# Two bias rows of a fused attention kernel: ScalarE copies into the PSUM banks in place of TensorE products with ones

## The reference

```python
qkv = x @ Wqkv.T + bqkv                       # here x is xn
q, k, v = jnp.split(qkv, 3, axis=-1)
...
scores = mask + scale * jnp.einsum('bnd,bmd->bnm', q, k)
attn = jax.nn.softmax(scores, axis=-1)
out = jnp.einsum('bnm,bmd->bnd', attn, v)
...
return out @ Wproj.T + bproj
```

## Time and profile before

| | us |
|---|---|
| median of 3 runs | 1820.19 |
| the profiled execution, its own time | 1821.34 |
| its span, first to last instruction | 1819.5 |
| TensorE (PE) busy | 1688.2 (93%), 8188 products |
| VectorE (DVE) busy | 1669.2 (92%) |
| GpSimd (POOL) busy | 1244.1 (68%) |
| ScalarE (ACT) busy | 787.5 (43%) |

### The profile page before, as it was taken

One profiled execution on the slowest core, in us unless ns is written; L12 is line 12 of the kernel. 1 busy time (PEld: TensorE's weight loads), 2 busy tenths in 40 slices (PEclk: granted clock), 3 DMA queues, 4 the chain that ended last, 5 costly groups with the idle time before them and its releaser, 6 DMA issues. The chain is left out here.

```text
span 1819.5 us, 26315 instructions
## 1 busy us (share of the span) xinstructions
PE 1688.2 (93%) x8188; PEld 823.3 (45%) x8188; DVE 1669.2 (92%) x1636; ACT 787.5 (43%) x1562; POOL 1244.1 (68%) x744
## 2 busy tenths in 40 slices
PE   3799999999999899999999999999999999999955
PEld 3344444444444444444444444444444444444422
DVE  4369999999999999999999999999999999999994
ACT  3544444444444444444444444444444434444311
POOL 3335858768585776958577586857759586776947
PEclk7899999999999999999999999999999999999977
DMA  6000111111111111111111111111111111110000
GB/s 231 1 1 24 35 47 36 47 37 41 41 36 48 36 47 35 47 37 35 47 36 47 37 36 47 36 48 36 42 41 41 43 35 47 36 47 18 26 21 29
DMA packets 40907, 75.33 MB, mean 41 GB/s; under 512 B 4912, under 2 KB 4912, under 8 KB 40752
## 3 DMA queue, kind: packets, MB, share of 16 engines
q1 hardware_dynamic: 40752, 73.43, 12.2%
HBM read 39.85 MB, written 33.55 MB: 40 GB/s over the span
## 5 line engine op out<-in xcount | busy, mean ns | idle before, releaser
L376 POOL TENSOR_TENSOR prod_pv<-kv,probs 128x2048 f32<-128x2048 f32 x192 | 811.2, 4237 | 130.1 <-DVE o_nat L677 117.4
L677 DVE TENSOR_REDUCE o_nat<-prod_pv 128x256 f32<-128x2048 f32 (+1 forms) x192 | 433.2, 2282 | 20.6 <-POOL prod_pv L376 11.9
L632 DVE TENSOR_REDUCE scores<-prod_qk 128x64 f32<-128x2048 f32 x192 | 439.3, 2288 | 7.3
L628 DVE TENSOR_TENSOR prod_qk<-q_ps,kv 128x2048 f32<-128x2048 f32 x192 | 431.9, 2249 | 0.0
L347 POOL TENSOR_TENSOR rstd<-var_eps,minus_half 128x1 f32<-128x1 f32 x128 | 70.3, 549 | 383.9 <-ACT var_eps L430 383.8
L451 ACT ACTIVATE kv<-v_ps 128x512 f32<-128x512 f32 x128 | 142.0, 1110 | 177.0 <-PE v_ps L504 177.0
L411 ACT ACTIVATE xT_hi<-xT_ps 128x512 f16<-128x512 f32 x128 | 76.4, 597 | 319.1 <-PE xT_ps L527 319.1
L504 PE MATMUL q_ps<-wqkv_hi,xT_hi 128*128 128x512 f16 x512 | 201.2, 393 | 0.0
L504 PE MATMUL q_ps<-wqkv_lo,xT_hi 128*128 128x512 f16 x512 | 200.9, 392 | 0.0
L504 PE MATMUL proj_ps<-wproj_hi,oT_hi 128*128 128x512 f16 x516 | 200.7, 389 | 0.0
L504 PE MATMUL proj_ps<-wproj_lo,oT_hi 128*128 128x512 f16 x516 | 200.7, 389 | 0.0
(11 more groups left out here) (136 smaller groups left out, 2461.6 us busy)
## 6 DMA issues: line engine op xcount, KB each, us to landing
xs<-in_L_attn_x SPq DMA_DIRECT2D x128, 256.0 KB, 2.6
out<-xs SPq DMA_DIRECT2D x128, 256.0 KB, 2.0
kv<-in_L_attn_Wqkv SPq DMA_DIRECT2D x3, 1024.0 KB, 10.2
kv<-in_L_ffn_weight SPq DMA_DIRECT2D x1, 1024.0 KB, 5.5
kv<-in_L_attn_Wproj SPq DMA_DIRECT2D x1, 1024.0 KB, 14.3
prod_pv<-in_L_attn_bqkv SPq DMA_DIRECT2D x2, 256.0 KB, 10.3
prod_pv<-in_L_attn_bproj SPq DMA_DIRECT2D x1, 256.0 KB, 9.3
prod_pv<-in_L_ffn_bias SPq DMA_DIRECT2D x1, 256.0 KB, 8.2
```

Of the source, the lines that this page charges most:

```text
L376: nc.gpsimd.tensor_tensor(o, v, p, ALU.mult).then_inc(pv_multiplied, 1)
L628: nc.vector.tensor_tensor(prod_qk[:, :].rearrange("p (m c) -> p m c", c=C), qb, k, ALU.mult).then_inc(qk_multiplied, 1)
L632: nc.vector.tensor_reduce(scores[:, :, m0:m0 + 4].rearrange("p h m -> p m h"), prod_qk[:, :].rearrange("p (m h d) -> p m h d", h=H, d=D), ...
L677: nc.vector.tensor_reduce(o_nat[:, n % 2, h * D:(h + heads) * D], prod_pv[:, u % 2, :].rearrange("p (c m) -> p c m", m=keys), AX_X, ALU.ad ...
```

## The change

The biases of the keys and the queries are no longer split into rows on GpSimd. They are loaded into two fp32 tiles of their own, `k_bias` and `q_bias`, and scaled there. ScalarE copies them into the banks (128 x 512 fp32, SBUF to PSUM), and TensorE's 12 products are added to what the bank holds. Three products in slot 5 (`banks_opened`) open the three banks once. The copy for the queries of slot j is ScalarE's first instruction of the slot, with the wait for `shifted_ready` that TensorE had; the copy for the next tile's keys stands behind the copy of the values out of their bank. The output bias keeps its row of ones.

```diff
-            nc.gpsimd.memset(k_bias_rows[:, :], 0.0).then_inc(consts_set, 1)
-            nc.gpsimd.memset(q_bias_rows[:, :], 0.0).then_inc(consts_set, 1)
...
-            nc.gpsimd.tensor_scalar(bk_all, bk_all, scale[:, 0:1], 1.0, ALU.mult, ALU.mult).then_inc(bias_steps, 1)
-            pool.wait_ge(bias_steps, 1)
-            split_into_rows(bk_all, k_bias_rows, 1, 0)
+            nc.gpsimd.tensor_scalar(k_bias[:, :], k_bias[:, :], scale[:, 0:1], 1.0, ALU.mult, ALU.mult).then_inc(k_bias_ready, 1)
             pool.wait_ge(bq_loaded, 16)
-            nc.gpsimd.tensor_scalar(bq_all, bq_all, scale[:, 0:1], 1.0, ALU.mult, ALU.mult).then_inc(bias_steps, 1)
-            pool.wait_ge(bias_steps, 7)
-            split_into_rows(bq_all, q_bias_rows, 7, 3)
+            nc.gpsimd.tensor_scalar(q_bias[:, :], q_bias[:, :], scale[:, 0:1], 1.0, ALU.mult, ALU.mult).then_inc(q_bias_ready, 1)
...
             def slot(i, j):
                 if at(i, j, L_TRANS):
                     high_parts(2 * KC, N_PARTS)
+                if at(i, j, L_KV):
+                    act.wait_ge(banks_opened, 1)
+                    act.wait_ge(k_bias_ready, 1)
+                    nc.scalar.activation(k_ps[:, :], k_bias[:, :], ACT.Copy).then_inc(k_preset, 1)
+                    act.wait_ge(q_bias_ready, 1)
+                if live(i, j, L_Q):
+
+                    n = j - L_Q
+                    after(act, shifted_ready, tile_count(i, n - 2))
+                    nc.scalar.activation(q_ps[n % 2][:, :], q_bias[:, :], ACT.Copy).then_inc(q_preset, 1)
                 if live(i, j, L_TRANS):
...
                     nc.scalar.activation(v_all[:, g % 2, :, n % N], v_ps[:, :], ACT.Copy).then_inc(v_kept, 1)
+                if live(i, j, L_KV) and live(i, j + 1, L_KV):
+                    after(act, k_kept, tile_count(i, j - L_KV))
+                    nc.scalar.activation(k_ps[:, :], k_bias[:, :], ACT.Copy).then_inc(k_preset, 1)
                 if live(i, j, L_SOFT):
...
             def slot(i, j):
                 if at(i, j, L_KV):
                     pe.wait_ge(w_ready, N_PARTS)
-                    pe.wait_ge(bias_rows_ready, 3)
+
+                    for b in (k_ps, *q_ps):
+                        last = nc.tensor.matmul(b[:, :], wqkv_hi[:, 0, 0:P], wqkv_hi[:, 0, 0:512], start=True, stop=True)
+                    last.then_inc(banks_opened, 1)
...
-                    after(pe, k_kept, tile_count(i, n - 1))
-                    nc.tensor.matmul(k_ps[:, :], ones[:, :], k_bias_rows[:, :], start=True, stop=False)
-                    split_products(k_ps, t_hi, t_lo, wqkv_hi, wqkv_lo, C, first=False).then_inc(k_summed, 1)
+                    after(pe, k_preset, tile_count(i, n))
+                    split_products(k_ps, t_hi, t_lo, wqkv_hi, wqkv_lo, C, first=False, preset=True).then_inc(k_summed, 1)
...
-                    after(pe, shifted_ready, tile_count(i, n - 2))
-                    nc.tensor.matmul(acc[:, :], ones[:, :], q_bias_rows[:, :], start=True, stop=False)
+                    after(pe, q_preset, tile_count(i, n))
                     split_products(acc, xT_hi[:, n % N, :], xT_lo[:, n % N, :], wqkv_hi, wqkv_lo, 0,
-                                   first=False).then_inc(q_summed, 1)
+                                   first=False, preset=True).then_inc(q_summed, 1)
```

More of the change, by code:

```diff
@@ L112, in attention_and_fp8_linear @@
         wffn_q = sb("wffn_q", [P, KC, C], BF16)
-        q_bias_rows = sb("q_bias_rows", [P, C], BF16)
-        k_bias_rows = sb("k_bias_rows", [P, C], BF16)
+        q_bias = sb("q_bias", [P, C], F32)
+        k_bias = sb("k_bias", [P, C], F32)
         out_bias_rows = sb("out_bias_rows", [P, C], BF16)
@@ L171, in attention_and_fp8_linear @@
         diagonals = kv[:, 15872:16064].bitcast(BF16).rearrange("p (a n) -> p a n", n=P)
-        bq_all, bk_all, bo_all, bffn_all = (prod_pv[:, 0, k * C:(k + 1) * C] for k in range(4))
+        bo_all, bffn_all = (prod_pv[:, 0, k * C:(k + 1) * C] for k in range(2))
         bias_rest = prod_pv[:, 1, 0:C]
@@ L195, in attention_and_fp8_linear @@
         bias_rows_ready = sem("bias_rows_ready")
+        k_bias_ready = sem("k_bias_ready")
+        q_bias_ready = sem("q_bias_ready")
+        banks_opened = sem("banks_opened")
+        k_preset, q_preset = (sem(n) for n in ("k_preset", "q_preset"))
         out_biases_scaled = sem("out_biases_scaled")
@@ L267, in _ @@
             sp.dma_start(bqkv_nat[:, :], bqkv.rearrange("(p j) -> p j", p=P)).then_inc(bqkv_loaded, 16)
-            sp.dma_start(bk_all, bqkv[C:2 * C].partition_broadcast(P)).then_inc(bk_loaded, 16)
-            sp.dma_start(bq_all, bqkv[0:C].partition_broadcast(P)).then_inc(bq_loaded, 16)
+            sp.dma_start(k_bias[:, :], bqkv[C:2 * C].partition_broadcast(P)).then_inc(bk_loaded, 16)
+            sp.dma_start(q_bias[:, :], bqkv[0:C].partition_broadcast(P)).then_inc(bq_loaded, 16)
             with nc.allow_non_contiguous_dma(reason="512 numbers, once"):
@@ L303, in _, with split_into_rows @@
                                            bass.bass_isa.ReduceOp.max).then_inc(amax_ready, 1)
-            def split_into_rows(b, rows, steps, ready):
+            def split_into_rows(b, rows):
                 hi, mid, low = bias_parts
                 nc.gpsimd.tensor_copy(hi, b).then_inc(bias_steps, 1)
-                pool.wait_ge(bias_steps, steps + 1)
+                pool.wait_ge(bias_steps, 2)
                 nc.gpsimd.tensor_tensor(bias_rest, b, hi, ALU.subtract).then_inc(bias_steps, 1)
-                pool.wait_ge(bias_steps, steps + 2)
+                pool.wait_ge(bias_steps, 3)
@@ L313, in split_into_rows @@
                 nc.gpsimd.tensor_copy(mid, bias_rest).then_inc(bias_steps, 1)
-                pool.wait_ge(bias_steps, steps + 3)
+                pool.wait_ge(bias_steps, 4)
                 nc.gpsimd.tensor_tensor(bias_rest, bias_rest, mid, ALU.subtract).then_inc(bias_steps, 1)
-                pool.wait_ge(bias_steps, steps + 4)
+                pool.wait_ge(bias_steps, 5)
                 nc.gpsimd.tensor_copy(low, bias_rest).then_inc(bias_steps, 1)
-                pool.wait_ge(bias_steps, steps + 5)
@@ L319, in split_into_rows @@
-                pool.wait_ge(consts_set, 6)
+                pool.wait_ge(bias_steps, 6)
+                pool.wait_ge(consts_set, 4)
                 for k, part in enumerate((hi, mid, low)):
                     nc.gpsimd.tensor_copy(rows[32 * k:32 * k + 1, :], part[32 * k:32 * k + 1, :]).then_inc(bias_rows_ready, 1)
-                    pool.wait_ge(bias_rows_ready, ready + k + 1)
+                    pool.wait_ge(bias_rows_ready, k + 1)
             pool.wait_ge(scales_ready, 1)
             pool.wait_ge(bk_loaded, 16)
-            nc.gpsimd.tensor_scalar(bk_all, bk_all, scale[:, 0:1], 1.0, ALU.mult, ALU.mult).then_inc(bias_steps, 1)
@@ L333, in _ @@
             pool.wait_ge(out_biases_loaded, 32)
             nc.gpsimd.tensor_tensor(bo_all, bo_all, bffn_all, ALU.add).then_inc(bias_steps, 1)
-            pool.wait_ge(bias_steps, 13)
+            pool.wait_ge(bias_steps, 1)
             nc.gpsimd.tensor_scalar(bo_all, bo_all, out_unscale[:, 0:1], 1.0, ALU.mult,
@@ L341, in slot @@
                     pool.wait_ge(out_bias_summed, 1)
-                    split_into_rows(bo_all, out_bias_rows, 13, 6)
+                    split_into_rows(bo_all, out_bias_rows)
                 if live(i, j, L_NORM):
@@ L498, in _, with split_products @@
                 last.then_inc(w_transposed, 1)
-            def split_products(acc, t_hi, t_lo, w_hi, w_lo, col, first=True):
+            def split_products(acc, t_hi, t_lo, w_hi, w_lo, col, first=True, preset=False):
                 parts = [(t, w, c) for c in range(KC) for t, w in ((t_hi, w_hi), (t_hi, w_lo))]
@@ L504, in split_products @@
                     last = nc.tensor.matmul(acc[:, :], t[:, c * P:(c + 1) * P], w[:, c, col:col + 512],
-                                            start=first and k == 0, stop=k == len(parts) - 1)
+                                            start=first and k == 0, stop=k == len(parts) - 1,
+                                            skip_group_check=preset)
                 return last
@@ L516, in slot @@
                     split_products(proj_ps, oT_hi, oT_lo, wproj_hi, wproj_lo, 0).then_inc(v_bias_projected, 1)
-                if at(i, j, L_Q):
-                    pe.wait_ge(bias_rows_ready, 6)
                 if at(i, j, L_PROJ):
-                    pe.wait_ge(bias_rows_ready, 9)
+                    pe.wait_ge(bias_rows_ready, 3)
                     pe.wait_ge(out_bias_summed, 1)
```

## The result

The changed kernel takes 1996.68 us (median of 4 runs, 1995.57 to 1998.43) against 1819.91 us for the kernel before beside it: a ratio of 1.097, 95% interval 1.0955 to 1.0993. The forecast was 1995.4 us. The profiled execution took 1997.41 us (span 1995.5), 176.0 us more span than before.

A forecast was written before the change was run, and what follows sets the result against it. VectorE was taken as the bound. Start -13.0, filling -3.0, waits for xT_q -7.0, longer slots +193.8 and drain +4.4 sum to +175.2 us, giving 1995.4 us against the median of 1820.19; range 1978 to 2053.

The forecast's parts named there:

- start: Before the first rstd: GpSimd's two splits of the biases go, making this part 13.0 us shorter.
- filling: Slots 5 to 12, where TensorE sets the pace: 13 products of 0.22 us go, taken as 3.0 us less.
- full pipe: chain less the 7.0 us: Slots 14 to 131: 112 slots longer by 1.73 us, 193.8 us, less 7.0 us of VectorE's waits for xT_q.
- drain: Slots 132 to 135: three slots longer by 1.24 us and one by 0.7, 4.4 us more.
- The bound: VectorE, not TensorE, sets the pace: its eight slots sum to 103.8 us against the stretch's 103.76.
- The moved wait: Head of ScalarE's slot: waiting for shifted there delays xT_hi, xT_q and VectorE's xT_lo, 1.73 us in 112 slots.
- the chain: Opening each full-pipe slot: shifted's end, queries' copy, xT_hi, xT_q, VectorE's start; 1.65 us, 1.73 with lost overlap.
- The copy for the keys: On ScalarE behind the values: about 0.5 us per slot, costing nothing; without the cover 0.5 per slot.
- The clock: TensorE's clock falls and becomes the bound if its mean is below 0.84: about 2196 us; chance 0.07.
- met in time: At ScalarE's first wait of a slot, shifted is already over, so only gains remain: 1797.2 us; chance 0.05.
- rows paying in full: TensorE, not VectorE, sets the pace, so 52 us come off the forecast: 1943 us; chance 0.05.

The follow-up runs named there:

- experiment 7: The kernel before with the two products of ones and biases left out and nothing in their place: 1808.42 us, ratio 0.9935.
- experiment 6: The changed kernel with four more products of 512 columns per tile on TensorE, overwritten by what follows: 2002.02 us, ratio 1.1001.
- experiment 3: The changed kernel with a second copy of q_bias, into a spare SBUF tile, ahead of the queries' copy and behind the same wait: 2055.72 us.
- experiment 2: The changed kernel with the wait for shifted left at the head of ScalarE's slot and the queries' copy moved behind the centring of xn: 1938.70 us.
- experiment 1: The changed kernel with the queries' copy and its wait moved on ScalarE from the slot's head to behind the centring of xn: 1796.54 us.
- experiment 10: As experiment 1, with GpSimd's scaling of the biases moved into slot 4, behind the first rstd: 1792.22 us, ratio 0.985.
- experiment 4: The changed kernel with xT_lo and oT_lo moved on VectorE behind the statistics and the sums: 1828.09 us, ratio 1.0047.
- experiment 5: As experiment 4, with the norm's two small values moved on ScalarE to the slot's head, ahead of the wait for shifted: 1803.67 us.
- experiment 9: The kernel before with GpSimd's work on the biases moved behind the first rstd: 1803.72 us, ratio 0.9905.

## Why the prediction was right

The time came out 1.3 us from the forecast. That closeness is in part luck: the mechanism held, but the four terms below are off by 1.6, 2.5, 1.9 and 2.1 us, and the errors nearly cancel. By the steps of its sum, on the spans of the two profiled executions:

| step | predicted | measured |
|---|---|---|
| start | -13.0 | -14.6 |
| filling | -3.0 | -0.5 |
| full pipe: chain less the 7.0 us | +186.8 | +188.7 |
| drain | +4.4 | +2.3 |
| sum | +175.2 | +176.0 |

**The bound.** Right: experiment 7 takes the rows away and gains 11.6 us, not 55; experiment 6 adds products to the full pipe at no cost. These two show it; the agreement of 103.8 with the stretch's 103.76 does not. The stretch of the earlier trace rows begins and ends inside slots, and from xT_lo to xT_lo (173.93 to 278.55) the same eight slots take 104.62 us.

**The moved wait.** Right in place, size and number. The full pipe has 112 waits for xT_q, 186.8 us in all; with 0.08 us of lost overlap each and less the 7.0 us from before, that makes 188.8; 188.7 were measured. Each link was within 0.04 us of its row: 0.03 + 0.53 + 0.48 + 0.59 + 0.03. The copy, for which there was no row, took 601 ns and held xT_hi back by 0.53 to 0.54, against 0.50 taken. By the Trainium skill (Perfetto Trace Analysis, Optimizing Scalar/DVE Operations) a ScalarE access costs less in PSUM than in SBUF, from which I had estimated 5 us less. The traces agree with the page's direction and not with my estimate. In experiment 3 and in the changed kernel a ScalarE copy of 128 x 512 stands first behind the same wait (groups by line: count, busy, mean ns, idle before):

```profile
L415 ACT ACTIVATE spare<-q_bias 128x512 f32<-128x512 f32 x128 | 80.6, 630 | 974.7 <-DVE shifted L721 974.7
...
L412 ACT ACTIVATE q_ps<-q_bias 128x512 f32<-128x512 f32 x128 | 77.0, 601 | 980.5 <-DVE shifted L717 980.5
```

From SBUF to SBUF it is 630 ns and from SBUF into PSUM 601. In experiment 2 xT_hi stands there, from PSUM to SBUF (fp16), with 597. So either side in PSUM saves about 30 ns. The copy gains on its write what it gives up on its read, so against the rows out of PSUM, on which the sum rested, nothing comes off. The six loop jumps did cover the chain: 17.5 us in six waits, as before.

**The start.** Right in kind: the first rstd is at 32.4 us instead of 46.9. 13.2 us of that are the two splits; the other 1.3 is GpSimd's first instruction on the biases, which started at 29.06 instead of 30.33, behind the same sort of "issue" wait. It started at 29.08 in experiment 7 too, whose start is that of the kernel before, so this part is not the change's; what sets it stays open.

**The filling: a term that was mis-sized.** It was forecast at -3.0 and came to -0.5 us, in three places. The first, 1.4 us, is slots 6 and 7. "The copy for the keys ... Nothing" holds in the full pipe and not there: TensorE waits for xn, and the keys' copy stands ahead of its scaling (L473) on ScalarE, in the timeline of ScalarE, 49 to 64 us:

```profile
58.27 1.09 ACT L458 ACTIVATE kv<-v_ps 128x512 f32<-128x512 f32 x1 [1.39 <-PE v_ps L514]
59.15 0.70 ACT L461 ACTIVATE k_ps<-k_bias 128x512 f32<-128x512 f32 x1
59.77 0.71 ACT L473 ACTIVATE xn<-xn,rstd 128x512 f32<-128x512 f32 x1
```

and of TensorE, 60 to 66 us:

```profile
60.53 0.66 PE L539 MATMUL xT_ps<-ident,xn 128*128 128x128 f32 x4 [1.44 <-ACT xn L473]
```

Before, such slots followed each other in 7.7 us and now in 8.1 to 8.3: the copy ate the row's 0.22 us and some 0.5 more.

The second place, 0.4 us, is slot 8: 9.49 us now, 9.55 before. There the queries' copy comes in ahead of xT_hi for the first time and shifts it once; in experiment 1, which has it elsewhere, this slot takes 9.12.

The third, 0.5 us, is slot 5. TensorE enters it at its lower level of 1.2 GHz after a wait, of 5.01 us before the change (granted 0.51 from 55.84 to 59.22) and of 3.56 us after (0.56 from 39.80 to 46.40). From its xT_lo to the next it had a mean granted clock of 0.95 and took 10.45 us before, and 0.90 and 10.71 after. With the same TensorE program experiment 1 had 0.98 and 9.89, experiment 10 had 1.00 and 9.24, so this part is the clock of one execution and not the change.

In slots 9 to 12 the queries' products hide the keys' copy, and the slots went from 9.50 to 9.07 us, the two rows exactly. In a pipe of 128 tiles all this is 2.5 us; in a short one it would not be small.

**The drain: the second mis-sized term.** It was forecast at +4.4 and came to +2.3 us. The 1.24 us per slot is right where it applies: from one `shifted` to the next, slots 134 and 135 grew by 1.27 each and slot 133 by 0.67, since this one, and not 132 as I had read, already waited 0.52 before. In slot 132 nothing was added, because the new wait took the place of one for GpSimd's product. VectorE in slot 132, before and after:

```profile
1711.03 2.29 DVE L677 TENSOR_REDUCE o_nat<-prod_pv 128x256 f32<-128x2048 f32 x1 [1.25 <-POOL prod_pv L376]
...
1881.79 0.69 DVE L672 TENSOR_TENSOR oT_lo<-oT_ps,oT_hi 128x512 f16<-128x512 f32 x1 [1.18 <-ACT oT_hi L425]
```

The rest, 0.8 us less between the last `shifted` and the end, is not explained.

**The rivals.** The clock did fall more often, as expected, and the full pipe's mean went from 0.99 to 0.96. The wait of 2.19 us before the queries in the timeline above was followed by this (windows, columns as above):

```profile
1011.50:1015.00 3.50, 3.50 (x11) 1.22 (x9) 2.84 (x4) 3.50 (x9) 1.68 (x3) 0.51 0.01 2
```

It cost nothing: no wait of VectorE in the full pipe ends with TensorE, 0.96 is far above the 0.84 from which it would have decided, and experiment 6 held the clock a little higher (0.97) and saved nothing. That lower clock follows idle time agrees with the Trainium skill (TensorE: Matmul & The Clock Gate, Part 1). The rival "met in time" was worked out at 1797.2 us, and experiment 1, which is that case made true, took 1796.5; so only its condition was not met. Its terms were near and not exact: with the same cuts experiment 1 has -14.3 us in the start, -1.9 in the filling, -6.2 in the full pipe and -2.6 in the drain, against -13.0, -3.0, -7.0 and nothing. The third, rows paying in full, fell with experiment 7.

## What to carry to other kernels

In a program that an engine executes in order, a wait is paid for by everything written behind it: before moving one, list what stands behind it and who waits for that in the same round. Here an instruction of 0.6 us and the wait in front of it cost 200 us at the head of ScalarE's slot and nothing eight instructions later. Taking work off an engine that is 93% busy brings only what its slack does not hide, 12 of 55 us here; read which engine's slots add up to the period before choosing what to relieve.

## What the runs showed that I had not expected

A cover can fail as soon as the thing that it hides behind is mended. GpSimd's lateness cost nothing in the changed kernel and 28.3 us in experiment 4, where the longer wait was gone; experiment 5 took 24.4 us of it back with two instructions of 0.22 us moved ahead of the wait.

TensorE waited 165.5 us for the queries' copy between 170 and 1900 us, where it had waited 39.5 us for `shifted` before, with no effect on the time (170 to 1700 us there). And the 16 us of experiment 9 had nothing to do with the bias rows as such: they were the price of GpSimd's program order in the start.
